# Exchange stage over edges packed into whole tiles by destination, stored tile by tile into the pair order

## The reference

```python
att,   v   = edge_msgs(K[row], Q[col], V[row], e1, e2)   # row = src, col = dst
att_i, v_i = edge_msgs(K[col], Q[row], V[col], e2, e1)
att   = seg_softmax(att, col, n)
att_i = seg_softmax(att_i, row, n)
agg = segment_sum([v * att, e0], col) + segment_sum([v_i * att_i, e0], row)
h = concat([agg, agg]); o = typed_linear(h, Wa, ba, node_type)
out = layernorm(x + layernorm_by_type(o + x))
```

## Time and profile before

| what | us |
|---|---|
| median of 3 runs (8218.47 to 8219.67) | 8218.89 |
| the profiled execution's own time | 8209.78 |
| its span, first to last instruction | 8208.1 |
| place, 424.5 to 2517.2 | 2092.7 |
| exchange, 2517.2 to 5513.0 | 2995.8 |
| softmax 0, 5513.0 to 5674.4 | 161.4 |
| aggregate 0, 5674.4 to 7056.0 | 1381.6 |

### The profile page before, as it was taken

How to read it: one execution, slowest core, us unless ns; L and a number is a source line. 1 busy time by engine, 2 the same in 40 slices (tenths; PEclk the granted TensorE clock), 3 DMA queues, 4 the chain that set the end, 5 groups by cost and what they waited for, 6 DMA issues and landing times. The chain is left out here.

```text
span 8208.1 us, 133262 instructions
## 1 busy us (share of the span) xinstructions
PE 5614.3 (68%) x34300; PEld 4034.9 (49%) x34301; DVE 6219.2 (76%) x9003; ACT 4454.8 (54%) x12726; POOL 5804.6 (71%) x6077
## 2 busy tenths in 40 slices
PE   7767767777776666676767676642677774299966
PEld 6456666666663333333333333322555553288854
DVE  8478988888887787887888778855666664588877
ACT  0134444444445666666666666633666663288845
POOL 3657777777777777777777777757777775088856
PEclk5866676667667888888888888876999997699987
DMA  2554443343336888888988888895999999899974
GB/s 77 187 179 135 130 146 113 111 132 111 111 111 211 294 291 296 294 294 290 297 294 294 294 290 298 291 217 205 393 389 388 389 387 218 58 287 287 288 243 117
DMA packets 1549522, 1936.30 MB, mean 236 GB/s; under 512 B 429993, under 2 KB 1354899, under 8 KB 1549083
## 3 DMA queue, kind: packets, MB, share of 16 engines
q1 hardware_dynamic: 1060126, 1029.14, 41.0%
q0 software_dynamic: 255392, 674.52, 25.8%
q10 hardware_dynamic: 233824, 230.96, 8.3%
HBM read 1090.09 MB, written 872.85 MB: 239 GB/s over the span
## 5 line engine op out<-in xcount | busy, mean ns | idle before, releaser
L1193 PE MATMUL exch_pG<-far_tab,exch_ohT 128*128 x3328 | 1625.5, 642 | 636.1 <-ACT exch_kc L1108 632.6
L1054 POOL DMA_INDIRECT exch_row<-table,exch_of x1664 | 1598.9, 961 | 553.9 <-issue 525.3
L1570 PE MATMUL sum_pS<-sum_row,sum_oh 128*128 128x260 f32 x6656 | 1619.6, 402 | 447.5 <-DVE edge_acc L1620 346.9
L940 POOL DMA_INDIRECT recs<-place_rec,place_addr x1568 | 1504.0, 959 | 583.2 <-issue 547.2
L1570 PEld LDWEIGHTS sum_pS<-sum_row,sum_oh 128*128 128x128 f32 x6656 | 1289.5, 199 | 777.3 <-DVE edge_acc L1620 422.0
L1193 PEld LDWEIGHTS exch_pG<-far_tab,exch_ohT 128*128 128x128 f32 x3328 | 745.3, 230 | 1465.1 <-issue 1420.1
L1268 POOL DMA_INDIRECT bys<-sum_pb x960 | 941.0, 980 | 312.9 <-issue 283.3
L1588 ACT ACTIVATE sum_off<-kept_ramp,sum_neg 128x128 f32<-128x128 f32 x3120 | 953.5, 387 | 98.6 <-POOL sum_neg L1525 98.6
L1107 ACT ACTIVATE exch_pb<-exch_pG 128x192 f32<-128x192 f32 x1664 | 552.2, 332 | 462.5 <-PE exch_pG L1193 395.0
L1268 POOL DMA_INDIRECT bys<-exch_pb x624 | 640.0, 1026 | 205.2 <-issue 160.9
L1610 DVE TENSOR_TENSOR sum_row<-sum_row,sum_pF 128x1792 f32<-128x1792 f32 x208 | 420.3, 2021 | 355.2 <-DMA sum_row<-spill 352.3
(11 more groups left out here) (324 smaller groups left out, 12031.1 us busy)
## 6 DMA issues: line engine op xcount, KB each, us to landing
bys<-place_none SPq DMA_DIRECT2D x52, 4224.0 KB
spill<-exch_row SPq DMA_DIRECT2D x208, 1024.0 KB
sum_row<-bys SPq DMA_DIRECT2D x208, 1024.0 KB
sum_row<-spill ACTq DMA_DIRECT2D x206, 1024.0 KB
mid<-exch_pb SPq DMA_DIRECT2D x208, 660.0 KB
sum_pb<-mid SPq DMA_DIRECT2D x192, 660.0 KB
exch_row<-table,exch_of POOLq DMA_INDIRECT x1664
recs<-place_rec,place_addr POOLq DMA_INDIRECT x1568
```

The source lines that it names most:

```text
L940: nc.gpsimd.indirect_dma_start(recs, bass.IndirectOffsetOnAxis(addr[:, par, t:t + 1], 0), rec[:, par, t, :], None).then_inc(s_scat[par], 16)
L1054: nc.gpsimd.indirect_dma_start(row[q][:, t, TD:TD + S.TW], None, table, bass.IndirectOffsetOnAxis(of[q][:, t:t + 1], 0)).then_inc(s_row[q] ...
L1193: nc.tensor.matmul(pG[t % 3][:, 0:GW], ohT[ring(j, 2)][:, t, :], flat[:, bass.ds(tiles[t] * GW, GW)], start=True, stop=True).then_inc(s_ga ...
L1570: last = nc.tensor.matmul(pS[j % SETS * HG + t // 2][:, 0:AW], oh[h][:, t, :], row[j][:, t, :], start=(t % 2 == 0), stop=(t % 2 == 1))
```

## The change

1. **Order 0 is filled to whole tiles.** An owner's edges begin at the next tile, not the next even one: with these inputs 1588 tiles belong to an owner, none without edges lies between them, and the exchange takes `NTD` = 1616 tiles, 202 steps (16 times 12 and a tail of 10), the last 28 tiles without edges. `recs` and `mid` are in this order.
2. **`spill` and `runs` stay in the pair order**, which the aggregate and the softmax need. A table `k.where` gives the place of each of order 0's tiles. SP loads 8 numbers from it into registers in each step, and stores each of the 8 tiles of `spill` (128 KB each) and of `runs` (2.5 KB each) by itself: 16 stores where there were 2.
3. **Places that no tile goes to are filled with "no edge"** in place, ahead of SP's loop: the tiles 1616 to 1663 of `spill` and of `runs`, one store each, and the last tile of each of 49 owners in both, 98 stores of one tile at addresses from registers.
4. **The table.** Project's DVE computes the shift of each owner (`pairs`), place's POOL fills a ramp (memset, iota), and the last part of place has three passes of `owners_of_tiles` where there were two, in bf16, with a matmul of 33 output rows that gives owner and place at once. `otile0` goes through memory.
5. **The exchange's one-hots.** `lows` writes f32 into PSUM (in the bank of the buffer `pQ1`) where it wrote bf16 to SBUF, and now runs for step n+2, within `gathered`, behind `owners(n + 1)`; `own_one_hots` reads it from PSUM and stands behind the slots (L1248), ahead of the queries (L1250), where it was first in the step.
6. **Forwards beside softmax 0:** 18 steps' tiles in 6 buffers (90), where there were 16 in 8 (80); aggregate 0 forwards 46 times 4 steps' (920) where there were 48 times 4 (960).

The diff, cut:

```diff
+        self.NTD = -(-((self.E + self.NO * (P - 1)) // P) // (2 * self.G)) * 2 * self.G
-        self.AHEAD = 16
-        self.EARLY = 8
+        self.AHEAD = 18
+        self.EARLY = 6
...
-def starts(nc, S, k, link, st, sti, zero, junk, stc, base, hs, pO):
+def starts(nc, S, k, link, st, sti, zero, junk, stc, base, hs, pO, whole):
-    link(nc.vector.tensor_scalar(sti[:], sti[:], 8, None, ALU.logical_shift_right))
-    link(nc.vector.tensor_scalar(st[:, 1, :], sti[:], 2.0, None, ALU.mult))
+    link(nc.vector.tensor_scalar(sti[:], sti[:], 6 + whole, None, ALU.logical_shift_right))
+    link(nc.vector.tensor_scalar(st[:, 1, :], sti[:], float(whole), None, ALU.mult))
...
+def pairs(nc, k, link, st, of, sti, zero, junk, c):
+    tot, begin = of[:, 4, :], of[:, 3, :]
+    NO = tot.shape[1]
+    link(nc.vector.tensor_scalar(sti[:], tot, float(2 * P - 1), None, ALU.add))
+    link(nc.vector.tensor_scalar(sti[:], sti[:], 8, None, ALU.logical_shift_right))
+    link(nc.vector.tensor_scalar(st[:, 0, :], sti[:], 2.0, None, ALU.mult))
+    link(nc.vector.tensor_tensor_scan(st[:, 1, :], st[:, 0, :], zero[:, 0:NO], 0.0, ALU.add, ALU.add))
+    link(nc.vector.tensor_tensor(st[:, 2, :], st[:, 1, :], st[:, 0, :], ALU.subtract))
+    link(nc.vector.tensor_tensor(st[:, 3, :], st[:, 2, :], begin, ALU.subtract))
+    nc.vector.tensor_scalar(c.last[:], st[:, 1, :], -1.0, 0.0, ALU.add, ALU.max)
...
             sp.wait_ge(s_none, 2)
+            SPILT, SCORED = none[:, 0:S.VW], none[:, S.SC:S.SC + S.H + 1]
+            sp.dma_start(spill[:, S.NTD:NT, :], bc(SPILT, 1, NT - S.NTD)).then_inc(s_blank, 16)
+            sp.dma_start(runs[:, S.NTD:NT, :], bc(SCORED, 1, NT - S.NTD)).then_inc(s_blank, 16)
+            for o in range(0, NO, 7):
+                _, ends = nc.values_load_multi_w_load_instructions(
+                    c.last[0:1, o:min(o + 7, NO)], engines=[nc.sync.engine], min_val=0, max_val=NT - 1,
+                    skip_runtime_bounds_check_because="an owner's last tile")
+                for end in ends:
+                    sp.dma_start(spill[:, bass.ds(end, 1), :], bc(SPILT, 1, 1)).then_inc(s_blank, 16)
+                    sp.dma_start(runs[:, bass.ds(end, 1), :], bc(SCORED, 1, 1)).then_inc(s_blank, 16)
             part = 0
             for g in range(2, NG):
...
             def owners_of_tiles(d):
+                pe.wait_ge(s_sel, 2)
                 pe.wait_ge(s_ge, d + 1)
-                    last = nc.tensor.matmul(to[0:1, 0:w], k.ones[0:NO, 0:1], flat[:, n * TC:n * TC + w], start=True, stop=True)
+                    last = nc.tensor.matmul(to[0:33, 0:w], sel[0:NO, :], flat[:, n * TC:n * TC + w], start=True, stop=True)
...
-    NS = NT // G
+    NS = S.NTD // G
...
-        lob = [s.sb(f"lob{n}", [P, G], BF16) for n in range(2)]
-        pQ = [s.pb(f"pQ{n}", [P, G, DK]) for n in range(2)]
+        pK = s.pb("pQ1")
+        pQ = [s.pb("pQ0", [P, G, DK])[:], pK[:, 0:G * DK].rearrange("p (t f) -> p t f", f=DK)]
+        low = pK[:, G * DK:G * DK + G]
...
+                _, where = nc.values_load_multi_w_load_instructions(
+                    k.where[0:1, bass.ds(n * G, G)], engines=[nc.sync.engine], min_val=0, max_val=NT - 1,
+                    skip_runtime_bounds_check_because="a tile's place")
                 sp.wait_ge(s_sinv, n + 1)
-                sp.dma_start(spill[:, bass.ds(n * G, G), :], row[q][:, :, 0:2 * TD + PROJ]).then_inc(s_v[q], 16)
+                for t in range(G):
+                    sp.dma_start(spill[:, bass.ds(where[t], 1), :], row[q][:, t:t + 1, 0:2 * TD + PROJ]).then_inc(s_v[q], 16)
                 sp.wait_ge(s_att, n + 1)
-                sp.dma_start(runs[:, bass.ds(n * G, G), :], at[h][:]).then_inc(s_as[h], 16)
+                for t in range(G):
+                    sp.dma_start(runs[:, bass.ds(where[t], 1), :], at[h][:, t:t + 1, :]).then_inc(s_as[h], 16)
...
             def lows(n, i, j):
-                act.wait_ge(s_oh, n - 1 if not isinstance(n, int) else max(n - 1, 0))
-                nc.scalar.activation(lob[ring(j, 2)][:], rec[q][:, :, S.LO], ACT.Copy).then_inc(s_lob, 1)
+                act.wait_ge(s_oh, n)
+                nc.scalar.activation(low, rec[q][:, :, S.LO], ACT.Copy).then_inc(s_lob, 1)
...
-            def gathered(n, j):
+            def gathered(n, i, j, more=True):
                 act.wait_ge(s_sco, n - 1 if not isinstance(n, int) else max(n - 1, 0))
+                if more:
+                    lows(n + 1, i, j + 1)
...
             def own_one_hots(n, j):
-                nc.vector.tensor_tensor(oh, bc(lob[h][:], 1, P), ramp8, ALU.is_equal).then_inc(s_oh, 1)
+                nc.vector.tensor_tensor(oh, bc(low, 1, P), ramp8, ALU.is_equal).then_inc(s_oh, 1)
...
             def step(n, i, j, left):
-                if left >= 2:
-                    own_one_hots(n + 2, j + 2)
...
                 nc.vector.tensor_tensor(pb[q][:, :, S.SLOTC].bitcast(I32), begin[:], mine[:, :, S.RANK], ALU.add)
+                if left >= 2:
+                    own_one_hots(n + 2, j + 2)
                 dve.wait_ge(s_ev, (n + 1) * G)
...
+    TURNS = (S.NTD // G - S.AHEAD) // 4
-            with pool.Fori(0, (NS - SKIP) // 4) as i:
+            with pool.Fori(0, TURNS) as i:
```

More of the change, by code:

```diff
@@ L525, in sort_edges @@
         c.stc = s.sb("stc", [P, 1])
+        c.stq = s.sb("stq", [P, 1])
+        c.shift = s.sb("shift", [P, 1])
+        c.last = s.sb("last", [P, NO], I32)
         c.base = s.sb("base", [P, S.LN, NO])
@@ L558, in starts, with place_edges @@
     link(nc.vector.tensor_reduce(stc[:, 0:1], junk[:], op=ALU.add, axis=AX))
-def place_edges(nc, k, S, edge_attr, recs, otile1, bys, e, table, w_time, b_time, c, Wa, wsum):
+def pairs(nc, k, link, st, of, sti, zero, junk, c):
[8 more added lines that the diff above has]
+    nc.vector.tensor_scalar(c.last[:], st[:, 1, :], -1.0, 0.0, ALU.add, ALU.max)
+    nc.vector.tensor_copy(st[:, 4, 0:1], st[:, 3, 0:1])
+    link(nc.vector.tensor_tensor(st[:, 4, 1:NO], st[:, 3, 1:NO], st[:, 3, 0:NO - 1], ALU.subtract))
+    for row, to in ((2, c.stq), (4, c.shift)):
+        link(nc.vector.tensor_tensor(junk[:], st[:, row, :], k.ident[:, 0:NO], ALU.mult))
+        link(nc.vector.tensor_reduce(to[:, 0:1], junk[:], op=ALU.add, axis=AX))
+def place_edges(nc, k, S, edge_attr, recs, otile0, otile1, spill, runs, bys, e, table, w_time, b_time, c, Wa, wsum):
     CT, SG, NO, NT, REC, LN, CE, REST = S.CT, S.SG, S.NO, S.NT, S.REC, S.LN, S.CE, S.REST
@@ L928, in _ @@
             dve.wait_ge(s_pre, 1)
-            starts(nc, S, k, link, st, sti, zero, stj, stc, first, hs, ahead)
+            starts(nc, S, k, link, st, sti, zero, stj, stc, first, hs, ahead, 2)
             nc.vector.tensor_copy(first_t[:].rearrange("p o l -> p l o"), first).then_inc(s_first, 1)
-            owners_of_tiles(1, stc, otile).then_inc(s_first, 1)
+            owners_of_tiles(2, stc, otile).then_inc(s_first, 1)
         @block.gpsimd
         def _(pool):
+            nc.gpsimd.memset(k.table[:], -1).then_inc(s_init, 1)
+            pool.wait_ge(s_init, 1)
+            nc.gpsimd.iota(k.table[32:33, :], pattern=[[1, NT]], base=0, channel_multiplier=0).then_inc(s_init, 1)
             def body(g, par, i, more):
@@ L1908, in gnn_resnorm @@
                 crd0 = Scope(nc, ctx3, "crd0").far("crd", [P, S.NT, S.H + 1])
-                softmax(nc, k, S, 0, crd0, load=runs, mid=mid, bys=bys)
+                softmax(nc, k, S, 0, crd0, load=runs, mid=mid, bys=bys, tiles=k.otile[0], of=otile0)
                 Scope.retire(nc)
```

85 lines of the change are left out of this document (53 added, 32 removed).

## The result

| | us |
|---|---|
| before, median of 4 runs (8211.37 to 8219.67) | 8218.7 |
| with the change, median of 4 runs (8327.06 to 8342.64) | 8335.5 |
| ratio, with its 95% interval | 1.0147 (1.0135 to 1.0159) |
| forecast | 8175 (8105 to 8290) |

A forecast was written before the change was run, and what follows sets the result against it. POOL was taken to bound the exchange, at 14.12 us a step. Place +76, exchange -81, softmax 0 +13 and aggregate 0 -52 sum to -44: 8209.8 to 8165.8, with 9.1 for the median 8175 us, range 8105 to 8290.

The forecast's parts named there:

- The pace of the exchange: Exchange, the 199 steps that remain: 14.2 us a step, +16 us, bounds -34 to +56.
- The loop: Exchange: scores' store must land and DVE reach the next scores within one step, 12.9 to 14.2 us.
- rival B: Exchange: the scores' loop sets the pace, step 14.8 us, +119, 8294 us; chance 0.19.
- the landing: Exchange, term of the scores' loop: time for the scores' store to land, 2.2 to 3.5 us.
- A tie: Exchange: the scores' loop and POOL tie at the loop's upper end, step taken as 14.2 us.
- The step count and the tail: Exchange: six steps go, three normal ones for -42 us and three without edges for -55 us.
- Place, the blanks: Place: "no edge" stores on SP's queue ahead of the weight halves, uncovered, +76 us, bounds 59 to 101.
- Softmax 0 and aggregate 0: Ten forwards more in softmax 0, +13 us; 40 fewer in aggregate 0, -52 us, bounds -37 and -58.
- The comparison: Exchange, DVE's one-hot: 1.14 us with an f32 operand in PSUM instead of 0.687, now ahead of the scores.
- C: Exchange: SP is the bound at 0.77 us a store, step 14.7, +100, and blanks +20: 8295 us; chance 0.06.
- D: Exchange: store lands in 2.5 us, POOL's collisions go, step 13.95; 8108 us with blanks at 59; chance 0.17.
- E: Exchange tail: nothing saved, as steps without edges drain in a fixed time; +40, 8215 us; chance 0.02.

The follow-up runs named there:

- the control: The kernel with the change, unchanged, run again beside the other runs: 8305.3 us, 1.0111 of the kernel before.
- pair with low places in SBUF: Kernel with the change, low places cast to bf16 in SBUF: 8228.3 us; the same with ACT's cast ahead of owners: 8167.4 us.
- the run on the kernel before: The kernel before with only the change's exchange one-hots (PSUM, cast behind owners, compared behind the slots): 8198.2 us, 0.9982 of the kernel before.

## Why the forecast was wrong, point by point

- **The pace of the exchange: the step that failed.** "I take 14.2 for the step: +0.08 x 199 = +16." It was 14.79. The loop had been found and laid out rightly, and rival B, chance 0.19, was this case with 8294. Of the sum's four terms three hold: 6.71 from owners to the scores' end (measured 6.69), 0.17 to SP (0.16), 3.8 to the last store (3.61).
  - The term that was mis-sized is the landing: bounds of 2.2 and 3.5 us, measured 4.07 in the first profile and 3.91 in the control. The upper bound was one row of a gather; over steps 4 to 199 of the same trace that interval has a median of 3.73 us. Nearer rows stood in the trace before: the landings of 3.42, 3.85 and 6.55 us for which owners itself waited in the first steps. With 3.85 the sum is 14.5 us, past the point where the prediction says that rival B makes the kernel slower. That the last of eight stores lands late because it stands behind fifteen others is not shown, and the single stores with 3.85 before and 4.09 to 4.85 in the run with one store speak against it.
  - A tie was counted as if it cost nothing. The pair with low places in SBUF puts it at 61 us for a loop with a median turn of 14.12.
  - That 6.71 met 6.69 so closely is in part luck. In the kernel before DVE did not wait for owners at that point; the 0.44 us from owners at 4012.29 to DVE's next operation at 4012.73 merely happen to match the 0.42 us that owners and the cast take ahead of the comparison.
- **The step count and the tail.** Forecast -42 and -55, -97 together. From the start of the reduction that makes the scores in the first step to that in the 197th (202nd before) there are 196 periods of 14.78 us instead of 201 of 14.07: five periods less are -70, the tail 122.6 us instead of 141.8, -19, the start +2: -87. The size is right. What makes a step without edges slow, one source row, was named in the forecast but not tried; the run with 128 source nodes showed it.
- **Place, the blanks.** Forecast +76 (59 to 101), measured 96.6. That nothing covers them was right. The small stores, 53 forecast, took 50 at 0.515; the large ones with the first register load took 33 instead of 18 and 0.75, and a register load takes 1.5 us in the median where 0.75 was put in with its moves.
- **Softmax 0 and aggregate 0.** +13 and -52 forecast, +13.8 and -45.6 measured; the mechanism is as said, and the 6 us that aggregate 0 fell short were not traced further.
- **The comparison.** 1.14 us by place's rows, 1.22 measured. That it would take the collisions away was right: the run on the kernel before gained 14 us and the mean forward fell from 1.027 to 0.995. The Trainium skill, "SBUF — State Buffer", section "Who interferes with whom", has a VectorE instruction with two SBUF inputs contend with a GpSimd instruction that reads SBUF, and one with at most one SBUF input, outside its two-port modes, not contend with GpSimd. That agrees with 97 of 252 against 0 of 343. The same section infers that a `tensor_tensor` does not hold up the making of descriptors; here indirect DMAs beside one took up to 0.2 us longer, so for these the measurement decides.
- **Rivals.** C (SP is the bound) fell: with four buffers SP issues the same stores and the step is 14.0. D's clean pace of 13.95 came true only with the loop open (13.97 with four buffers, by POOL's groups). The prediction's own rows account for only part of that: three forwards at 1.0 instead of 1.027 make 14.04; the rest came from the gathers, at 0.956 instead of 0.961, and from forwards at 0.995. D's landing of 2.5 us did not come. E fell too: the tail became 19 us shorter with the tiles.
- **Sum.** Of the 161 us between forecast and result the pace is 123 (139 less 16), place 21, the tail and the count 10, aggregate 0 6, and softmax 0 1.

What stays open: what sets the landing of 3.7 to 4.1 us, and why it differs between occasions (4.07 and 3.91 for the same kernel) and between kernels with the same exchange stage.

## What to carry to other kernels

When an operation is moved earlier on one engine and its input comes from an engine that waits for a landing, write down the loop that this closes and count in how many steps the landing may come: from two to one made a store's landing the pace of 202 steps, and one more buffer, or two operations exchanged, opened it again. Take the price of a landing from an operation that waited for just that store, be it in three steps of 208. A loop that ties with the bound is a loss to be expected, since a landing varies and only its delays count. And before work is taken out because it is slow, see why it is: here the padding asked for one row 128 times, and giving it other rows gained 35 us with one added instruction.

## What was not expected of the hardware

- A register load took SP 1.50 us in the median in place (7 of 0.97 to 3.99) and 1.63 in the exchange (202 of 0.52 to 2.24), while PE's takes 0.59 in the median.
- Gathers of 128 rows that are all the same row: in the last steps of the exchange POOL is idle for 47.0 + 22.4 us in the kernel before; with 128 different rows it is 17.1 + 14.9, and more gathers are done.
- A bf16 comparison on DVE with both operands in SBUF stretched gathers and forwards on POOL that it overlapped: 97 of 252 took over 1.1 us, and none of 343 with an f32 operand in PSUM.
- A store of 6 MB from broadcast rows, with that of 6144 rows of 20 bytes behind it, held up the whole place stage by 30 us; in twelve parts between the groups the two cost nearly nothing (place 2101.4 us, with all blanks, against 2093.3 without any).
